# Output unit 5 fed with its state products directly, and two more normalisation blocks on ScalarE

## What is computed

```python
x = _layernorm(x + attention(x))
for t in range(8):                       # the same 512 rows of each batch element
    ft = sigmoid(x[t] @ wf.T + c @ uf.T + bf)
    it = sigmoid(x[t] @ wi.T + c @ ui.T + bi)
    gt = tanh(x[t] @ wc.T + c @ uc.T + bc)
    c = ft * c + it * gt
h = tanh(x @ wo.T + c @ uo.T + bo)        # the last state, for all t
x = _layernorm(x + h)
```

## Time and profile before

| what | value |
|---|---|
| median of 3 runs | 102.27 us (102.12 to 102.87) |
| the profiled execution's own time | 102.38 us |
| its span, first to last instruction | 100.4 us |
| mean granted TensorE clock | 0.986 of full speed |
| busy PE / PEld / DVE / ACT / POOL | 91.0 / 78.5 / 80.6 / 68.5 / 41.5 us |
| units' stores: 7 of 256 KB, 2 of 128 KB | 2.2 and 2.0 us to landing (medians) |

### The profile page before, as it was taken

How to read it: one execution, slowest core, us unless ns; L and a number is a source line. 1 busy time by engine, 2 the same in 40 slices (tenths; PEclk the granted TensorE clock), 3 DMA queues, 4 the chain that set the end, 5 groups by cost and what they waited for, 6 DMA issues and landing times.

```text
span 100.4 us, 1923 instructions
## 1 busy us (share of the span) xinstructions
PE 91.0 (91%) x607; PEld 78.5 (78%) x607; DVE 80.6 (80%) x235; ACT 68.5 (68%) x143; POOL 41.5 (41%) x62
## 2 busy tenths in 40 slices
PE   5998999999799999999999999999999999986700
PEld 4778879689388978878898899999799999775300
DVE  3255498979999997799589989998836999999970
ACT  1446679479387784967669445769675859899760
POOL 3006398327547238207504802443020056456850
PEclk9999999999999999999999999999999999999995
DMA  1868999100000000000000000000000000143366
GB/s 34 294 214 304 404 390 372 46 0 3 0 0 0 0 0 0 3 7 0 0 0 0 0 0 7 0 3 3 7 0 0 0 0 0 53 162 104 104 209 209
DMA packets 5413, 7.36 MB, mean 73 GB/s; under 512 B 507, under 2 KB 3228, under 8 KB 5404
## 3 DMA queue, kind: packets, MB, share of 16 engines
q1 hardware_dynamic: 4972, 6.92, 19.1%
q10 hardware_dynamic: 432, 0.33, 1.4%
HBM read 5.15 MB, written 2.10 MB: 72 GB/s over the span
## 4 chain that ended last, share of the span: by engine, by line
PE 56%; DVE 28%; ACT 6%; issue 5%; POOL 2%; DVEq 0%; ACTq 0%; POOLq 0%
PE ps_ctx L442 7%; PE ps_k L419 7%; PE ps_q L433 6%; PE ps_ctx L462 5%; DVE stats L1151 5%; PE ps_f L406 4%; DVE x L1140 3%; DVE x L970 3%; DVE x L1167 3%; PE ps_x L476 2%; DVE s L1021 2%; DVE x L985 2%; DVE new L1014 2%; PE ps_ctx L452 2%; PE ps_ctx L453 2%
## 5 line engine op out<-in xcount | busy, mean ns | idle before, releaser
L355 POOL TENSOR_TENSOR s_lo<-s,s_hi 128x512 fp32r<-128x512 f32 (+1 forms) x7 | 7.4, 1056 | 24.9 <-ACT s_hi L766 24.9
L342 POOL TENSOR_TENSOR rstd<-var_eps,minus_half 128x4 f32<-128x4 f32 (+1 forms) x9 | 9.1, 1011 | 11.9 <-DVE var_eps L1159 11.9
L326 POOL TENSOR_TENSOR rstd<-var_eps,minus_half 128x4 f32<-128x4 f32 x8 | 8.6, 1079 | 6.6 <-DVE var_eps L961 6.5
L317 POOL TENSOR_TENSOR k_pair<-k_rows 128x256 f32<-128x256 f32 x8 | 6.3, 784 | 9.1 <-DVE k_rows L996 9.1
L970 DVE TENSOR_SCALAR x<-x,stats,rstd 128x128 f32<-128x128 f32 x26 | 10.0, 441 | 0.0
L815 ACT ACTIVATE x_hi<-ps_x 128x512 fp32r<-128x512 f32 x8 | 4.8, 595 | 6.2 <-PE ps_x L476 6.2
L419 PE MATMUL ps_k<-wkq,x_cols 128*128 128x128 f32 x64 | 8.9, 284 | 0.0
L736 ACT ACTIVATE k_exp<-ps_k,minus_one 128x512 f32<-128x512 f32 x8 | 5.5, 687 | 4.8 <-PE ps_k L427 3.9
L419 PEld LDWEIGHTS ps_k<-wkq,x_cols 128*128 128x128 f32 x64 | 8.3, 201 | 0.4 <-DMA wkq<-w_kq 0.3
L433 PE MATMUL ps_q<-x_cols,wkq 128*128 128x512 f32 x16 | 8.2, 593 | 0.0
L985 DVE SCALAR_TENSOR_TENSOR x<-ps_ctx,z_inv,x_rows 128x128 f32<-128x128 f32 x28 | 8.0, 342 | 0.1
(11 more groups left out here) (209 smaller groups left out, 285.0 us busy)
## 6 DMA issues: line engine op xcount, KB each, us to landing
x_cols<-xt SPq DMA_DIRECT2D x8, 256.0 KB, 7.2
x_rows<-x SPq DMA_DIRECT2D x8, 256.0 KB, 7.1
out<-x SPq DMA_DIRECT2D x7, 256.0 KB, 2.2
wgate<-w_gate SPq DMA_DIRECT2D x1, 384.0 KB, 6.6
out<-x SPq DMA_DIRECT2D x2, 128.0 KB, 2.0
wkq<-w_kq ACTq DMA_DIRECT2D x1, 131.0 KB, 3.6
wvo_in<-w_vo_in ACTq DMA_DIRECT2D x1, 128.0 KB, 3.4
wout<-w_out SPq DMA_DIRECT2D x1, 128.0 KB, 6.8
```

Source lines behind the costliest of these rows:

```text
L317: nc.gpsimd.tensor_tensor(k_pair[:], k_rows[:, a % 2, 0:C // 2], k_rows[:, a % 2, C // 2:C], ALU.add).then_inc(k_pair_ok, 1)
L326: nc.gpsimd.tensor_tensor(rstd[:, b], var_eps[:, b], minus_half[:], ALU.pow).then_inc(rstd_ok, 1)
L342: nc.gpsimd.tensor_tensor(part_of(rstd, u, T), part_of(var_eps, u, T), minus_half[:, 0:nt * H].rearrange("p (t c) -> p t c", c=H), ALU.pow ...
L355: nc.gpsimd.tensor_tensor(s_lo[:, t % 2, part], state(t)[:, part], s_hi[:, t % 2, part].bitcast(F32), ALU.subtract).then_inc(slo_ok[k], 1)
```

## The change

Unit 5 moves from PRELOADED to DIRECT. On ScalarE `preload(5)`, a copy of 512 columns, goes. On TensorE unit 5 gets a bias pass of 512 columns and four matmuls of the state, and these and the products of x for unit 5 now stand ahead of `out_g(1)`. The wait for the bank ps_f moves with it from ScalarE to TensorE. On ScalarE the tanh of unit 5 now stands ahead of `preload(6)`, `normalise(2)` ahead of the tanh of unit 4, `normalise(3)` ahead of the tanh of unit 6, and `normalise(4)` ahead of the tanh of unit 8. VectorE normalises one block of units 3 and 4 in place of two, and ScalarE three in place of two.

```diff
-DVE_NORM = [1, 1, 1, 2, 2, 2, 0, 2, 2]
+DVE_NORM = [1, 1, 1, 1, 1, 2, 0, 2, 2]
...
-DIRECT = (0, 4)
-PRELOADED = (5, 6, 7, 8)
+DIRECT = (0, 4, 5)
+PRELOADED = (6, 7, 8)
...
                 if u == 4:
                     pe.wait_ge(w_ok, 1)
+                if u == 5:
+                    pe.wait_ge(w_ok, 2)
...
             out_x(4)
+            out_x(5)
+            out_s(4)
+            out_s(5)
             out_g(1)
-            out_s(4)
-            out_x(5)
             out_x(6)
...
                 act.wait_ge(g_mm, 2)
-                if u == 5:
-                    act.wait_ge(w_ok, 2)
                 if u == 6:
...
             normalise(1)
-            preload(5)
+            normalise(2)
             out_tanh(4)
+            out_tanh(5)
             preload(6)
-            out_tanh(5)
-            normalise(2)
             preload(7)
             preload(8)
+            normalise(3)
             out_tanh(6)
-            normalise(3)
             out_tanh(7)
+            normalise(4)
             out_tanh(8)
-            normalise(4)
             normalise(5)
```

## The result

The kernel after takes 103.11 us, the median of 9 runs (102.81 to 103.63); the kernel before takes 102.60 beside it (9 runs, 102.12 to 102.87). The ratio is 1.0056, with a 95% interval of 1.0029 to 1.0082: slower by about 0.6%, and less than the 1% that was called no change. The medians differ by 0.51 us. The profiled execution took 103.10 us, with a span of 101.0 and 2.1 around it.

A forecast was written before the change was run, and what follows sets the result against it. VectorE looked like the bound, but ScalarE's unbroken list ahead of unit 6's tanh was taken to decide; 2.83 us there against 2.21, plus 0.04, made 0.66 later: 102.27 + 0.66 = 102.93 us, range 102.3 to 103.5.

The forecast's parts named there:

- Step 1: TensorE, units 4 and 5: bias pass and moved products fall into a wait and cost only 0.04 us.
- Step 2: TensorE, g: it ends at 89.74 us instead of 87.20, 2.54 us later for units 6, 7 and 8.
- Step 4: ScalarE, tanh of unit 5 to that of unit 6: 2.83 us against 2.21, unit 6's tanh 0.66 later.
- Step 5: TensorE, unit 6: x products end 0.36 us ahead of the tanh, costing nothing; unit 6 is ready 0.66 later.
- Step 6: VectorE before unit 6's statistics: free at 92.64 us, it then waits 1.1 us, so the relief falls into a wait.
- Step 7: The tail: everything behind unit 6's statistics, last stores included, moves by 0.66 us; unit 8's tanh has 0.32 cover.
- the prediction's own sign: At the kernel's end: the prediction is wrong if the end moves by another amount than the statistics of unit 6.
- A: VectorE stays the bound and its relief comes through: end 0.47 us earlier, 101.80 us; chance 0.05.
- B: The two limits on unit 6's statistics meet, ScalarE absorbing part: loss under 0.35 us, about 102.4; chance 0.13.
- C: TensorE's clock falls from 2.4 to 1.2 GHz behind g: 2.2 us later, 104.4 us; chance 0.08.
- D: Tail cover is thinner than 0.32 us, unit 4's third block delays unit 8's tanh: 0.66 + 0.4, 103.3; chance 0.06.

The follow-up runs named there:

- the second trace: The kernel after, unchanged, timed and traced once more beside the kernel before: 103.31 us against 102.47, ratio 1.0087.
- The two experiments on unit 3: Kernel after with the old sharing of blocks (units 3 and 4), ratio to before 1.0012; kernel after with unit 3's blocks behind unit 6's tanh, 1.0023.
- The first experiment: Kernel before with one block each of units 3 and 4 left unnormalised on VectorE: 103.08 us, ratio 1.0048; run again, 102.34 us, 0.9984.

## Why the prediction was right

The forecast was 102.9 us, 0.66 above before, in a range of 102.3 to 103.5. Measured are 103.11, and from the anchor 0.70 us at the last store (0.62 in the second trace). The forecast stood on a kernel before of 102.27, which took 102.60 in the comparison: the medians rose by 0.51 us there and by 0.84 the second time. The 0.66 lies between, but such medians are too coarse to confirm it; the traces do. Its steps one by one, against the trace of the kernel after:

- Step 1, TensorE. Right. The x products of unit 5 start at 85.88 and take the place of the wait; its state products end at 87.89 + 1.06 = 88.95. From the anchor the tanh of unit 4 starts 0.13 later than before (0.04 forecast; 0.06 in the second trace). The sum had two prices here that nearly cancel: a bias pass costs 0.32 (85.88 - 85.56) and not 0.23, and the x products ahead of one 0.81 (86.69 - 85.88) and not 0.93, as the earlier trace rows has them too (85.68 - 84.87 = 0.81); together 0.06 more. The tanh of unit 5 starts 0.03 later, in the second trace 0.05 sooner. VectorE made up for the 0.13 with the block of unit 3 that it no longer has. ScalarE from there on:

```profile
85.64 2.41 ACT L793 ACTIVATE x<-x,shift,rstd 128x128 f32<-128x128 f32 x6
88.09 0.58 ACT L788 ACTIVATE ps_q<-ps_q 128x512 f32<-128x512 f32 x1
88.99 0.58 ACT L788 ACTIVATE ps_f<-ps_f 128x512 f32<-128x512 f32 x1 [0.31 <-PE ps_f L574]
89.56 0.58 ACT L781 ACTIVATE ps_c<-ps_i 128x512 f32<-128x512 f32 x1
90.05 0.64 ACT L781 ACTIVATE ps_ctx<-ps_i 128x256 f32<-128x256 f32 x2
90.58 1.27 ACT L793 ACTIVATE x<-x,shift,rstd 128x128 f32<-128x128 f32 x3
91.73 0.60 ACT L788 ACTIVATE ps_c<-ps_c 128x512 f32<-128x512 f32 x1
```

- Step 2, g 2.54 us later. Right: its bias pass ended at 87.20 before (80.11 from the anchor) and ends at 89.15 + 0.36 = 89.51 (82.58), 2.47 later.
- Step 4, the term that decides. From the tanh of unit 5 to that of unit 6: 91.73 - 88.99 = 2.74 us, against 2.83 forecast and 2.21 before. By parts: tanh and wait 0.57 (0.61), copy of 512 0.49 (0.51), copies of 256 0.53 (0.56), three blocks 1.15 (1.15). With the 0.03 of the tanh of unit 5 the loss is 0.56 where 0.66 stood. The second trace has 2.75. These rows answer to the earlier trace rows.
- Step 5. Right, with cover: the x products of unit 6 end at 90.28 + 1.13 = 91.41, 0.32 ahead of the tanh (0.36 forecast). The two experiments on unit 3 show the next limit just there: as soon as the blocks go, these products hold the tanh.
- Step 6. Right: VectorE waits 0.92 us (1.1 forecast). The first experiment shows the same from the other side: VectorE's relief alone leaves the statistics of unit 6 where they were.
- Step 7. The cover of unit 8 was 0.23 (0.32 forecast). One term was missing: the root on GpSimd, 1.01 before, took 1.10, so that 0.60 at the statistics became 0.69 at VectorE's last blocks. It made up for the 0.10 by which step 4 was too large, and that was luck. By the prediction's own sign the end was not to move by another amount than the statistics; it did, by these 0.09 us. The step's remark that the last stores move by the same amount held (0.70), but it treated them as a fixed tail, and dividing one of them brought 0.42 us.

Of the rivals, A (VectorE stays the bound) is refuted by the first experiment. B (a loss under 0.35 us) by the traces of both runs of the kernel after. C, the fall of the clock: TensorE was idle for 0.76 us ahead of unit 6 and again for 0.53, and the granted clock stayed at 1.00, its level of 2.4 GHz, from 86.30 to 98.00 us. By the rule of the Trainium skill ("TensorE: Matmul & The Clock Gate", section "HAM oscillation — how this bites in real kernels") waits between bursts can cost the clock; the trace shows no fall behind waits of this size. D (unit 8) didn't come in.

The figures of the Trainium skill's page "ScalarE: Activation LUTs", section "Rules for kernel authors", gave 0.41 us for a block (an estimate); ScalarE's distance from block to block is 1.15 / 3 = 0.38 again, so the rows decide for 0.38.

## What to carry to other kernels

When two chains reach the same instruction within a tenth of a microsecond, relieving the engine that is busy 96% of the time brings nothing until the other chain is shortened too; follow that one back to where an engine has no wait, and count what stands ahead of it in the list. An operation that is taken out of an engine's wait is worth nothing, and the same operation placed where the engine never waits costs its full length (the copy, 0.49 us here). At the end of a kernel look at when the last large transfer can begin and how many bytes stand behind it, before looking at who issues the last one.

## What was not expected of the hardware

- The start scatters by more than the change is worth: the first `k_rows` on VectorE began between 6.68 and 8.04 us in twelve profiled executions of kernels whose lists up to there are the same. One kernel timed twice gave 1.0048 and 0.9984. The two jobs ran on different chips; what in the loading differs, and whether the chip has a part in it, was not tried.
- The power on GpSimd over 128 x 4 elements took 1.01 us in most traces where it followed the shift at once and 1.10 to 1.19 behind most waits; but in every trace it also took 1.01 once behind a wait of about 1.55 us, and with the store of unit 6 by ScalarE it took 1.11 with no wait shown, so the wait alone isn't the cause. It stays open.
- With the store of unit 6 issued by ScalarE, the last three stores, issued at 97.66 and later, moved no data until about 98.5 us, and then at some 345 GB/s together; issuing the last of them 0.39 us sooner changed nothing.
